# Half-row scores and maxima products, a narrow turn of the output, and a new place for every unit of the softmax stage

## What is computed

```
scores = einsum('bhqd,bhkd->bhqk', qh, kh) / sqrt(8)      # where the mask is 0: -1e9
attn = softmax(scores, axis=-1)
context = einsum('bhqk,bhkd->bhqd', attn, vh)
x = x + tanh(g_xattn[1]) * (context @ W_o.T + b_o)
```

## Time and profile before

| what | value |
|---|---|
| median of 3 runs | 790.48 us (790.0 to 791.91) |
| profiled execution | 790.32 us, span 788.5 us |
| granted TensorE clock, mean | 0.965 of 2.4 GHz |
| busy share of the span | TensorE 86%, VectorE 68%, ScalarE 65%, GpSimd 34% |
| copies of O (L993), one for each window | first at 267.4, last at 671.3 us |

### The profile page before, as it was taken

How to read it: one execution, slowest core, us unless ns; L and a number is a source line. 1 busy time by engine, 2 the same in 40 slices (tenths; PEclk the granted TensorE clock), 3 DMA queues, 4 the chain that set the end, 5 groups by cost and what they waited for, 6 DMA issues and landing times.

```text
span 788.5 us, 19444 instructions
## 1 busy us (share of the span) xinstructions
PE 679.7 (86%) x7276; PEld 475.0 (60%) x7283; DVE 534.8 (68%) x1252; ACT 510.0 (65%) x807; POOL 270.4 (34%) x322
## 2 busy tenths in 40 slices
PE   3599899986369889889889889889899999799997
PEld 2477777764226555555555655555566666468777
DVE  5799999998778768678768768768767771311122
ACT  4477777776226777687776777777778768343531
POOL 3388888883233222222231241241242010000000
PEclk9899999999589999999999999999999999799999
DMA  4122222254524736626625724734744670110110
GB/s 137 39 79 79 78 84 94 94 153 29 112 73 89 172 74 127 154 54 127 152 71 111 166 77 92 166 93 84 158 118 94 124 169 15 48 43 28 54 40 24
DMA packets 59377, 74.40 MB, mean 94 GB/s; under 512 B 35320, under 2 KB 40178, under 8 KB 59306
## 3 DMA queue, kind: packets, MB, share of 16 engines
q1 hardware_dynamic: 59306, 73.39, 39.4%
HBM read 32.35 MB, written 1.40 MB: 43 GB/s over the span
## 4 chain that ended last, share of the span: by engine, by line
PE 51%; DVE 10%; issue 7%; ACT 4%; POOL 2%; DVEq 0%; ACTq 0%; POOLq 0%
PE ps L734 10%; PE ps L649 7%; PE ps L807 6%; PE ps L795 6%; DVE mx L1574 6%; PE ps L641 6%; PE ps L721 5%; PE ps L635 4%; PE ps L669 2%; ACT P L985 1%; ACT KP L928 1%; POOL Qb L1109 1%; DVE silu L1480 1%; ACT Vp L911 1%; ACT silu L943 1%
## 5 line engine op out<-in xcount | busy, mean ns | idle before, releaser
L985 ACT ACTIVATE P<-ps,kbias,kscale 125x896 f32<-125x896 f32 x192 | 210.5, 1098 | 91.5 <-PE ps L721 88.8
L1574 DVE TENSOR_REDUCE mx<-ps 128x1 f32<-128x500 f32 x336 | 215.5, 673 | 78.4 <-PE ps L649 74.6
L649 PE MATMUL ps<-KP,Qb 128*128 128x500 bf16 x336 | 129.0, 386 | 5.4 <-DVE mx L1574 4.3
L734 PE MATMUL ps<-P,Vp 125*32 125x112 f32 x3072 | 113.8, 266 | 1.6 <-ACT P L985 1.1
L734 PEld LDWEIGHTS ps<-P,Vp 125*32 125x32 f32 x3072 | 67.4, 109 | 51.6 <-issue 30.0
L1095 POOL TENSOR_TENSOR KP<-kvall,KP 128x1500 bf16<-128x1500 f32 x16 | 48.5, 3032 | 141.1 <-ACT KP L928 141.1
L526 PE MATMUL ps<-wkv,cT 128*125 128x256 f32 x384 | 91.8, 383 | 1.0 <-ACT arena L885 1.0
L526 PEld LDWEIGHTS ps<-wkv,cT 128*125 128x125 f32 x384 | 69.3, 190 | 9.9 <-issue 1.3
L885 ACT ACTIVATE arena<-ps,arena 125x128 f32<-125x128 f32 x192 | 54.8, 368 | 27.9 <-DVE arena L1279 13.9
L721 PE MATMUL ps<-QS,KS 128*128 128x112 bf16 x768 | 69.8, 214 | 3.3 <-issue 1.9
L721 PE MATMUL ps<-QS,arena 128*128 128x112 bf16 x768 | 67.5, 213 | 5.0 <-issue 5.0
(11 more groups left out here) (212 smaller groups left out, 1010.2 us busy)
## 6 DMA issues: line engine op xcount, KB each, us to landing
cT<-ctxT_dram SPq DMA_DIRECT2D x32, 750.0 KB, 4.2
KS<-KP SPq DMA_DIRECT2D x48, 375.0 KB, 7.2
arena<-KP SPq DMA_DIRECT2D x48, 375.0 KB, 7.4
QS<-QD SPq DMA_DIRECT2D x96, 28.0 KB, 5.6
wgu<-w_dram SPq DMA_DIRECT2D x8, 256.0 KB, 3.1
silu<-w_dram SPq DMA_DIRECT2D x8, 256.0 KB, 2.8
x<-xh_dram SPq DMA_DIRECT2D x1, 512.0 KB, 3.6
mixed<-att SPq DMA_DIRECT2D x16, 28.0 KB
```

The lines of the kernel that those rows point to most:

```text
L649: ins = nc.tensor.matmul(ps[:, bank, 0:KCW], q[:, 128 * c:128 * c + 128], KP[par][0][:, KCW * k:KCW * k + KCW], start=True, stop=True)
L734: ins = nc.tensor.matmul(ps[r:r + PW, 7, c:c + PAIRW], Vp[par][0:TK, t, p, :], P[t % 2][0:TK, PAIRW * p:PAIRW * p + PAIRW], start=(t == 0 ...
L985: nc.scalar.activation(P[t % 2][0:TK, :].rearrange("p (k n) -> p k n", k=2), src, ACT.Exp, scale=kscale[0:TK, bass.ds(n, 1)], bias=kbias[0 ...
L1574: ins = v.tensor_reduce(mx[:, c, k:k + 1], ps[:, bank, 0:KCW], AX.X, ALU.max)
```

## The change

Every score product now works on one half of the 128 rows. Even heads have their stacked rows on partitions 0 to 63, odd heads on 64 to 127; half k of a step makes eight products of 64 rows, 128 keys and 56 query columns, all on the rows of parity k. The masked query copies shrink from two blocks of 56 columns to one, and the shifts stand in rows 0 and 64 of QS. The columns of Qb are ordered by parity, so that 18 of the 21 maxima products need 64 rows only: MX0, MX2, ... MX16, which follow the first half of the scores, use rows 0 to 63, and MX1, MX3, ... MX17, which follow the weighing, rows 64 to 127. MX18 to MX20 keep 128 rows. All still have 500 columns and 128 results.

OT multiplies by 36 picked columns of the identity instead of 128, and Vp holds a second column of ones for the odd head. OT and DE move to the side bank and G to the alternating ones. The units get new places; Q1 moves to the window that follows. ScalarE's key_part2 moves from step 10 to step 1 of the next window, GpSimd's key_part3 with it to the head of its window. VectorE's rest of K2 moves behind SH, and its copy of the shifts waits for the stacked transfers. On GpSimd the first two passes over the pair of windows are written out. Left out of the diff are the removal of the pmask input, its wait count, and the order of the columns of hmask1.

```diff
@@ -29,6 +29,7 @@
+OTW = 64
@@ -44,7 +45,6 @@
-ONES = 0
@@ -54,27 +54,29 @@
+BLOCKS = ([(c + 4 * h, k, HALF * h, HALF) for c in range(CH // 2) for k in range(KC) for h in range(2)]
+          + [(CH // 2, k, 0, 128) for k in range(KC)])
...
-    [[["MX0"], ["V0"], ["MX1"]], [["MX2"], ["AT"], ["MX3"]], [["MX4"], ["OT"], ["MX5"]],
-     [["MX6"], ["V1"], ["MX7"]], [["MX8"], ["DE"], ["MX9"]], [["MX10"], ["FT"], ["MX11"]],
-     [["MX12"], ["K0"], ["MX13"]], [["MX14"], ["FO"], ["MX15"]], [["MX16"], ["K1"], ["MX17"]],
-     [["MX18"], ["XT", "K2"], ["MX19"]], [["MX20"], ["V2"], []], [["SH"], [], ["G"]]],
-    [[["MX0"], ["V0"], ["MX1"]], [["MX2"], ["U"], ["MX3"]], [["MX4"], ["OT"], ["MX5"]],
+    [[["MX0"], ["Q1"], ["MX1"]], [["MX2"], [], ["AT", "MX3"]], [["MX4"], ["OT"], ["MX5"]],
+     [["MX6"], ["V0"], ["MX7"]], [["MX8"], ["DE"], ["MX9"]], [["MX10"], ["K0"], ["MX11"]],
+     [["MX12"], ["V1"], ["MX13"]], [["MX14"], ["K1"], ["MX15"]], [["MX16"], ["FT"], ["MX17"]],
+     [["MX18"], ["K2"], ["XT", "MX19"]], [["MX20"], ["V2"], ["G"]], [["SH"], [], []]],
+    [[["MX0"], ["FO"], ["MX1"]], [["MX2"], ["V0"], ["U", "MX3"]], [["MX4"], ["OT"], ["MX5"]],
...
-     [["MX12"], ["K1"], ["MX13"]], [["MX14"], ["DN", "ET"], ["MX15"]], [["MX16"], ["K2"], ["MX17"]],
-     [["MX18"], ["V2"], ["MX19"]], [["MX20"], ["LT"], []], [["SH"], [], ["Q1"]]],
+     [["MX12"], ["V2"], ["DN", "MX13"]], [["MX14"], ["K1"], ["MX15"]], [["MX16"], ["ET"], ["MX17"]],
+     [["MX18"], ["K2"], ["MX19"]], [["MX20"], ["LT"], []], [["SH"], [], []]],
...
-ON_SIDE = ["AT", "G", "HT", "LT", "Q1"] + LAST
+ON_SIDE = ["AT", "DE", "HT", "LT", "Q1", "OT"] + LAST
...
-LOOPED = (1, 5)
+LOOPED = (2, 5)
@@ -87,6 +89,10 @@
+def in_chain(i, unit):
+    return unit in CHAIN and (1 <= i <= CHAIN_PAIRS if unit == "Q1" else i < CHAIN_PAIRS)
@@ -101,7 +107,7 @@
-                                     or (i >= CHAIN_PAIRS and u in CHAIN)))]
+                                     or (u in CHAIN and not in_chain(i, u))))]
@@ -298,12 +303,12 @@
-        QD = [[sb(f"QD{n}_{k}", [128, 2, S], BF16) for k in range(3)] for n in range(2)]
+        QD = [[sb(f"QD{n}_{k}", [128, S], BF16) for k in range(3)] for n in range(2)]
...
-        QS = [sb(f"QS{n}", [128, HQ], BF16)[:] for n in range(2)]
+        QS = [sb(f"QS{n}", [128, HQ2], BF16)[:] for n in range(2)]
@@ -439,7 +444,7 @@
-                                 QD[par][part][:].rearrange("p k s -> p (k s)")).then_inc(sem(f"stacked{par}"), 16)
+                                 QD[par][part][:]).then_inc(sem(f"stacked{par}"), 16)
@@ -641,13 +646,13 @@
-                    c, k = divmod(int(unit[2:]), KC)
-                    if c == 0 and k == 0:
+                    c, k, r, n = BLOCKS[int(unit[2:])]
+                    if unit == MXS[0]:
...
-                    ins = nc.tensor.matmul(ps[:, bank, 0:KCW], q[:, 128 * c:128 * c + 128],
-                                           KP[par][0][:, KCW * k:KCW * k + KCW], start=True, stop=True)
+                    ins = nc.tensor.matmul(ps[:, bank, 0:KCW], q[r:r + n, 128 * c:128 * c + 128],
+                                           KP[par][0][r:r + n, KCW * k:KCW * k + KCW], start=True, stop=True)
@@ -657,17 +662,19 @@
-                                r = ONES + 32 * k
+                                r = HALF * k
...
+                    wanted = ident[:].rearrange("p (q n) -> p q n", q=4)
...
-                            lhs = O[:, PAIRW * c + S * k:PAIRW * c + S * k + S]
-                            ins = nc.tensor.matmul(ps[HALF * par:HALF * par + S, bank, 128 * (2 * c + k):128 * (2 * c + k) + 128],
-                                                   lhs, ident[:], start=True, stop=True)
+                            lhs, at0 = O[:, PAIRW * c + S * k:PAIRW * c + S * k + S], OTW * (2 * c + k) + DK * (1 - k)
+                            lo = (DK + 1) * k
+                            ins = nc.tensor.matmul(ps[HALF * par:HALF * par + S, bank, at0:at0 + 4 * (DK + 1)],
+                                                   lhs, wanted[:, :, lo:lo + DK + 1], start=True, stop=True)
@@ -716,11 +723,11 @@
-                for p in range(4 * k, 4 * k + 4):
+                rows = slice(HALF * k, HALF * k + HALF)
+                for p in range(NPAIR):
...
-                    ins = nc.tensor.matmul(ps[:, 2 * (t % 2) + k, PAIRW * (p % 4):PAIRW * (p % 4) + PAIRW],
-                                           KS[par][:, c0:c0 + 128], QS[par][:, PAIRW * p:PAIRW * p + PAIRW],
-                                           start=True, stop=True)
+                    ins = nc.tensor.matmul(ps[:, 2 * (t % 2) + k, S * p:S * p + S], KS[par][rows, c0:c0 + 128],
+                                           QS[par][rows, S * p:S * p + S], start=True, stop=True)
@@ -729,10 +736,10 @@
+                heads = P[t % 2][0:TK, :].rearrange("p (k q s) -> p q k s", k=2, q=NPAIR)
...
-                    ins = nc.tensor.matmul(ps[r:r + PW, 7, c:c + PAIRW], Vp[par][0:TK, t, p, :],
-                                           P[t % 2][0:TK, PAIRW * p:PAIRW * p + PAIRW],
+                    ins = nc.tensor.matmul(ps[r:r + PW, 7, c:c + PAIRW], Vp[par][0:TK, t, p, :], heads[:, p, :, :],
@@ -744,7 +751,7 @@
-                                 else i + 2 if unit in CHAIN else w + 1)
+                                 else i + 1 if unit == "Q1" else i + 2 if unit in CHAIN else w + 1)
@@ -989,7 +996,7 @@
-                    act.wait_ge(sem("aux_ready"), filled(prev(at), "OT"))
+                    act.wait_ge(sem("side_ready"), filled(prev(at), "OT"))
@@ -1015,7 +1022,7 @@
-                                    chain(at, unit, i + 2)
+                                    chain(at, unit, i + (1 if unit == "Q1" else 2))
@@ -1024,10 +1031,8 @@
-                        if t == 1 and fixed(i) and w == 0:
-                            key_part2(1, 1)
-                        if t == T - 2 and "K2" in has:
-                            key_part2(w + 2, par)
+                        if t == 1 and not (fixed(i) and w == B - 1):
+                            key_part2(w + 1, 1 - par)
@@ -1064,7 +1069,8 @@
-                ins = nc.gpsimd.memset(Vp[n][:, :, :, 0:1], 1.0)
+                nc.gpsimd.memset(Vp[n][:, :, :, 0:1], 1.0)
+                ins = nc.gpsimd.memset(Vp[n][:, :, :, 1 + 2 * DK:2 + 2 * DK], 1.0)
@@ -1120,9 +1126,8 @@
-                    ins = nc.gpsimd.tensor_tensor(QD[par][k][:], bc(QP[k][:, z, HALF * par:HALF * par + S], 1,
-                                                                    [128, 2, S]),
-                                                  bc(pmask[:], 2, [128, 2, S]), ALU.mult)
+                    ins = nc.gpsimd.tensor_tensor(QD[par][k][:], QP[k][:, z, HALF * par:HALF * par + S],
+                                                  onesf[:, 0:S], ALU.mult)
@@ -1160,31 +1165,35 @@
-            key_part3(1, 1)
...
-                for par in range(2):
-                    b = 2 * i + par + 2
-                    if par == 0 and not (fixed(i) and i == 0):
-                        parts(i + 1)
-                        biased(i + 1)
-                    queries(b, par, i + 1, prev((i, par)))
-                    if par == 0 and chained:
-                        deviation(i + 2, 0)
-                        deviation(i + 2, 1)
-                    if par == 0 and not (fixed(i) and i == 0):
-                        last_deviation(i - 1)
-                    if par == 1 and chained:
-                        deviation(i + 2, 2)
-                    key_part3(b, par)
...
-            pair1(0)
+                first = fixed(i) and i == 0
...
+                key_part3(2 * i + 1, 1)
+                if chained:
+                    deviation(i + 2, 0)
+                    deviation(i + 2, 1)
+                if not first:
+                    parts(i + 1)
+                    biased(i + 1)
+                queries(2 * i + 2, 0, i + 1, prev((i, 0)))
...
+                key_part3(2 * i + 2, 0)
+                queries(2 * i + 3, 1, i + 1, (i, 0))
+                if not first:
+                    last_deviation(i - 1)
+                if chained:
+                    deviation(i + 2, 2)
...
+            for i in range(LOOPED[0]):
+                pair1(i)
...
+            key_part3(B - 1, 1)
@@ -1568,34 +1577,36 @@
-                    c, k = divmod(int(unit[2:]), KC)
-                    if c == 0 and k == 0 and not (fixed(b) and b == 0):
+                    c, k, _, _ = BLOCKS[int(unit[2:])]
+                    if unit == MXS[0] and not (fixed(b) and b == 0):
...
+                    dve.wait_ge(sem(f"stacked{par}"), loads(b, par, 2 * STACK))
...
-                        r = ONES + 32 * k
-                        ins = v.tensor_copy(QS[par][ONES:ONES + 1, HQ2 * k:HQ2 * k + HQ2],
-                                            ps[r:r + 1, bank, 0:HQ2])
+                        r = HALF * k
+                        ins = v.tensor_copy(QS[par][r:r + 1, :], ps[r:r + 1, bank, 0:HQ2])
...
-                dve.wait_ge(sem("aux_ready"), filled(at, "OT"))
```

(50 more changed lines are left out.)

## The result

The changed kernel takes 782.55 us, median of four runs (777.32 to 784.85), against 791.19 us for the kernel before on the same chip: a ratio of 0.988, 95% interval 0.9831 to 0.9929. Its profiled execution took 784.56 us, span 782.8 us.

A forecast was written before the change was run, and what follows sets the result against it. TensorE was taken to lead, not alone; a chained window was to lose 3.4 us (1.5 TensorE, the rest waits). Twelve such windows gave -41, with the last four -41 together, from 790.3 to 749 us; own range 732 to 766, overall 728 to 785.

The forecast's parts named there:

- C: Rival: half-row scores don't pass a longer maxima product, so a half step's times add to 0.42 us; 784 us, chance 0.14.
- a microsecond of TensorE counted at two thirds: Chain of waits in a window pair: TensorE's lines about two thirds, so -2.3 us a window counts as -1.5.
- the narrow turn: OT on 36 columns instead of 128: eight products 0.051 us shorter each, 0.4 us of TensorE a window.
- seven turns of 0.093: Tiling turns around MX18 to MX20 on all rows, among 18 x 0.093 = 1.7 us a window.
- 3.6 us of overlap less 1.0 of turns: Scores beside MX0 to MX17: 18 x 0.20 = 3.6 us saved a window, against turns between tilings.
- rival B: Overlap works, but waits take its place (late keys or bursts of reductions): windows of 27 us, 766 us, chance 0.14.
- Waits: Waits removed by new banks and places, outside TensorE's own saving: 1.9 us a window.
- three moves: OT to the side bank 0.74 us; G's bank and Q1's window 0.55; K2's rest behind SH 0.6.
- The price of a pair: Weight load plus 64-row product of 56 columns on TensorE: taken as 26 ns, between about 25 and 49.
- the floor of the stacked keys: Key cast, subtraction, transfers and shift copy after step 1: a window cannot fall below about 24.2 us.
- the unhidden cast: ScalarE's key_part2 in step 1, taken as zero; up to 1.45 us without room; part of the range's upper end, 766.
- D: Slower rival: a 64-row load-and-product pair costs 49 to 50 ns and the halves add up; 860 us, chance 0.12.

The follow-up runs named there:

- x2: Changed kernel with only the 21 maxima products ahead of the first window on 128 rows: 780.5 us, ratio 0.9834 to the kernel before.
- x16: Changed kernel with 14 added products (128 rows by 500 columns) filling TensorE's idle gap behind window 14's last step: 778.35 us, ratio 0.9855.
- x13: Changed kernel with full-row maxima products ahead of the first window, 14 bridging products behind window 14, key_part2 at step 0 in window 14: 772.95 us, ratio 0.9758.
- x3: Placement alone: changed kernel with scores and maxima products on 128 rows as before; new places, banks and narrow turn kept: 773.19 us, ratio 0.9754.
- x10: Placement alone (full-row scores and products) with half the exponentials' columns and half the keys in the maxima left out: 759.63 us, ratio 0.9585.
- x9: Changed kernel with half the exponentials' columns and half the keys in the maxima left out: 765.6 us, ratio 0.9669 to the kernel before.
- x4: Changed kernel with VectorE taking each maximum over 250 of 500 keys: 771.69 us, ratio 0.9666 to the kernel before.
- x15: Placement alone (full-row scores and products) with OT on 128 identity columns as before: 780.23 us, ratio 0.9842 to the kernel before.
- x1: Changed kernel with all 21 maxima products on 128 rows again, scores kept on 64 rows: 842.62 us, ratio 1.0651 to the kernel before.
- x6: Changed kernel with one more 128-row by 500-column product in each of 11 steps of the last window: 792.74 us, ratio 1.002.

## Why the prediction was wrong

**The direction and the range were right, the size was not.** The median of 782.55 us lies in the range only because that reaches up to C's 784, and C's mechanism is refuted by the timeline, so the nearness to 784 is chance. The profiled execution is 35.6 us above the forecast. By the table of windows: 12.3 us in windows 1 to 10 (2.17 against 3.4 us each), 5.6 ahead of the first, 6.1 in window 0, 3.7 in window 11, 6.3 in the last four and 1.2 behind; the rest is rounding.

**The missing term: the clock.** The sum took every price at the clock of its row and had no term for a change of that clock, and no rival had one. Stretches at 1.2 GHz add up to 115 us after and 58 before. x2 and x16 show two of them with their causes, 4.9 us ahead of the first window and 6.5 us in window 15, and x13 that both together, with the earlier keys, are worth 9.6 us in the medians. Window 0 was not settled: it takes 29.7 us in x2 as well and 28.1 in placement alone. In window 11 the kernel after has 10 us at half clock from 563.7 and takes 28.6 us, x13 none and 25.9 us, but x16 has none either and takes 27.3: the clock can be part of it only, and what else it is stays open.

**The step that failed in the steady windows: a microsecond of TensorE counted at two thirds.** TensorE's busy time fell by 2.1 us a window as forecast, and of this the narrow turn showed whole (0.49 us, forecast 0.4 at two thirds). The half rows took 1.4 us and showed 0.3 to 0.45. The share of an engine in the chain says how often it is the last to finish, not how far the next one is behind. Where the rest went can be read from the distances between the first scores of neighbouring steps (sums for a window, mean of windows 1 to 10, us):

| steps | before | placement alone (x3) | after | full rows, both omissions (x10) | half rows, both omissions (x9) |
|---|---|---|---|---|---|
| 0 to 8 | 21.65 | 19.99 | 19.08 | 19.35 | 17.84 |
| 9 and 10 | 4.69 | 4.70 | 5.44 | 4.56 | 5.40 |
| 11 | 2.54 | 2.30 | 2.20 | 2.20 | 2.26 |

In steps 9 and 10 three maxima products on all rows stand between half-row scores, and the half rows cost 0.74 us there; the prediction's seven turns of 0.093 for these steps, 0.65, were about right. What was wrong is the gain in steps 0 to 8: 3.6 us of overlap less 1.0 of turns, 2.6 us of TensorE's time, gave 0.9. In these steps the first halves (from the first scores of a step to those of its second half) take 3.88 us together against 4.69. That is 1.9 us of waiting above nine undisturbed halves of 0.22, where placement alone has 1.0 above nine of 0.41. TensorE's loads for maxima products waited for reductions on VectorE (total us in 270 to 540 us, times, longest) in the kernel after, then in placement alone:

```profile
PEld ps L654 <- DVE mx L1583: 12.0, 30, 0.7
```

```profile
PEld ps L655 <- DVE mx L1585: 3.3, 10, 0.4
```

So in the steady windows rival B came nearest: the overlap works, waits take its place, and 26.7 us stand against its 27. Half the reductions give 0.8 us back (x4), half the exponentials 0.35, both 1.2. With both left out the half rows gain 1.5 us in steps 0 to 8 and lose 0.8 in steps 9 and 10, which makes the 0.6 us between x10 and x9, though the busy time differs by 1.3. The end of each wait was not tried alone.

**Waits.** 1.9 us a window were forecast without the turn's own 0.4, and x15, placement with the wide turn, gives 1.4. Which of the three moves gave less was not tried.

**Right.** The price of a pair, 26 ns; the overlap; the turn between tilings; windows 12 and 13, 24.2 and 24.8 us forecast and, between the copies of O as in the forecast, 24.6 and 24.7 measured; and the floor of the stacked keys, 24.2 us, with 24.4 measured for window 14 between exponentials (25.1 between the copies) and VectorE waiting 5.2 us for a transfer there. The sum did not use that floor: it lets window 14 grow by 1.3 us from 21.7, to 23.0, where the floor asks for 2.5. The ends of the forecast's own range don't follow from their terms either: twelve windows of 24.2 us give 735 and not 732, and the unhidden cast with TensorE's gain at half gives windows of 27.2 and 771 us, not 26.8 and 766. C and D are refuted by the timeline: scores that follow a longer product are recorded beside it, 26 ns apart, and the next product starts 0.23 us after the first (415.53 to 415.76). The strict reading of the Trainium skill's rule on order (TensorE: Matmul & The Clock Gate, Part 3, The mechanism) does not hold back short products on other rows; whether their ends keep the order can't be read from modelled ends.

## What to carry to other kernels

Packing products into the two halves of the array brought a half step from 0.41 to 0.22 us wherever nothing waited, but the kernel then spent 115 us at 1.2 GHz instead of 58: price the change at both clocks, look for idle gaps of some microseconds ahead of stretches that hold only packed products, and compare the granted clock slice by slice, not the mean alone. A few products left on all rows among packed ones can take back most of the gain: here 0.7 of 0.9 us a window. Before counting an engine's saving at its share of the chain, find by how much the next engine is behind, step by step; and try the reordering without the new arithmetic, which here was the better kernel. A transfer chain that is moved later needs its floor worked out for the shortest window as well as for the usual one.

## What the runs showed of the hardware

- Eight products of 64 rows by 56 columns are recorded beside one of 500 columns on the other rows, 26 ns apart, their weight loads with them, and the next product of 500 columns starts 0.23 us after the first.
- A turn between products on 64 and on 128 rows costs about 0.1 us each way: 0.32 and 0.31 us in place of 0.21 (x1). The turn from scores to weighing on 32 columns costs 0.09.
- Ahead of the first window, maxima products on half of the rows, with TensorE 73% busy, left it at 1.2 GHz for 25 us; the same products on all rows had it at 2.4 GHz (x2). With shorter reductions between them the half-row products had it back 14.5 us earlier (x4).
- Half-row scores with weighing stayed at 1.2 GHz through window 15, 99% busy for 21 us, and at 2.4 GHz for the whole window, 90% busy, when they began there (x16). One product of 128 rows by 500 columns a step did not change it (x6).
